# One core, gated cross-attention with a mixture of experts: four expert weight sets parked in DRAM at every second step, three split in place late

## What is computed

```python
# x: 4 x 512 x 256, ctx: 4 x 1024 x 256; 16 heads of 16; all fp32
x = x + tanh(g_xattn) * attention(layernorm(x), ctx, ctx, Wq, bq, Wk, bk, Wv, bv, Wo, bo)
x = x + tanh(g_ffn) * ffn(layernorm(x))
# ffn: 1 shared expert + 8 routed experts, top 2 of softmax(x @ gate_w + gate_b)
#   expert(z) = (silu(a) * b) @ w2 + b2,  a, b = split(z @ w1 + b1), w1: 256 x 512, w2: 256 x 256
```

## Time and profile before

| | us |
|---|---|
| median of 3 runs | 699.52 |
| the three runs | 698.99, 699.52, 710.46 |
| the profiled execution's own time | 703.27 |
| its span, first to last instruction | 701.4 |
| its mean granted TensorE clock, share of full speed | 0.963 |

### The profile page before, as it was taken

One profiled execution on the slowest core, in us unless ns is written; L12 is line 12 of the kernel. 1 busy time (PEld: TensorE's weight loads), 2 busy tenths in 40 slices (PEclk: granted clock), 3 DMA queues, 4 the chain that ended last, 5 costly groups with the idle time before them and its releaser, 6 DMA issues.

```text
span 701.4 us, 12642 instructions
## 1 busy us (share of the span) xinstructions
PE 627.2 (89%) x3577; PEld 324.4 (46%) x3577; DVE 482.6 (69%) x804; ACT 424.1 (60%) x842; POOL 281.0 (40%) x318
## 2 busy tenths in 40 slices
PE   4996867999999999999999999999986989999990
PEld 3774632333323323232233333336455768888870
DVE  4788876888887878778688888856675664444430
ACT  4775343777767767677677777786641414555540
POOL 2443242424834654464321113311037532655642
PEclk9999896999999999999999999999998999999995
DMA  8999889565587679569556745005069556665645
GB/s 239 359 263 369 174 266 179 88 106 108 121 218 204 154 153 229 170 116 250 138 83 80 105 66 161 1 13 229 2 219 317 187 196 140 100 104 101 94 46 142
DMA packets 83607, 110.29 MB, mean 157 GB/s; under 512 B 16798, under 2 KB 64841, under 8 KB 82604
## 3 DMA queue, kind: packets, MB, share of 16 engines
q1 hardware_dynamic: 70268, 78.34, 47.3%
q0 software_dynamic: 13296, 31.42, 17.6%
HBM read 64.19 MB, written 47.34 MB: 159 GB/s over the span
## 4 chain that ended last, share of the span: by engine, by line
PE 64%; issue 12%; DMA 8%; POOL 6%; DVE 6%; ACT 1%; POOLq 1%; another core or an unknown queue 0%; SPq 0%; ACTq 0%; DVEq 0%
PE psO L1535 15%; PE psS L1508 15%; PE psM L1490 12%; PE psH L1752 8%; DMA kq<-msb 6%; PE psY L1778 4%; POOL parts L603 3%; PE psH L1709 2%; PE psX L1603 1%; PE psX L1741 1%; PE psH L1763 1%; POOL kq L596 1%; PE psO L1578 1%; PE psM L1508 1%; DMA wA_raw<-wqkv 1%
## 5 line engine op out<-in xcount | busy, mean ns | idle before, releaser
L1142 DVE TENSOR_REDUCE mneg<-psM 128x1 f32<-128x1024 f32 x240 | 282.7, 1219 | 73.8 <-PE psM L1490 73.6
L876 ACT ACTIVATE pr<-psS 128x512 f32<-128x512 f32 x488 | 266.7, 595 | 108.0 <-PE psS L1508 107.9
L1508 PE MATMUL psS<-kq 99*128 99x512 bf16 x488 | 153.0, 387 | 12.7 <-DMA kq<-msb 12.1
L1535 PE MATMUL psO<-pr,vt 128*32 128x512 f32 x1024 | 136.9, 607 | 0.0
L1490 PE MATMUL psM<-kq 96*128 96x512 bf16 x480 | 128.5, 388 | 4.4 <-DVE mneg L1142 2.7
L1508 PEld LDWEIGHTS psS<-kq 99*128 99x128 bf16 x488 | 40.0, 97 | 161.1 <-ACT pr L876 131.3
L585 POOL TENSOR_TENSOR msb<-mcp,none 16x128 bf16<-16x128 f32 x16 | 6.2, 389 | 198.0 <-ACT mcp L853 198.0
L783 POOL DMA_INDIRECT acc<-ysb,ids x39 | 60.2, 1543 | 61.1 <-ACT ysb L999 42.6
L1490 PEld LDWEIGHTS psM<-kq 96*128 96x128 bf16 x480 | 46.7, 98 | 63.6 <-DVE mneg L1142 8.1
L1752 PE MATMUL psH<-wall,zgT 128*128 x234 | 61.0, 396 | 1.4 <-DVE zgT L1373 1.4
L1379 DVE TENSOR_TENSOR rg<-psH,rs 128x256 f32<-128x256 f32 x39 | 16.6, 425 | 57.2 <-ACT rs L987 52.7
(11 more groups left out here) (250 smaller groups left out, 845.2 us busy)
## 6 DMA issues: line engine op xcount, KB each, us to landing
kq<-k_parts SPq DMA_DIRECT2D x96, 128.0 KB, 6.4
wall<-w_parts SPq DMA_DIRECT2D x7, 1536.0 KB
w_parts<-wraw POOLq DMA_DIRECT2D x11, 768.0 KB, 4.9
v_pad<-vst SPq DMA_DIRECT2D x16, 512.0 KB, 8.6
vt<-v_pad SPq DMA_DIRECT2D x16, 512.0 KB, 10.2
k_parts<-parts SPq DMA_DIRECT2D x16, 384.0 KB, 7.1
kq<-q_parts SPq DMA_DIRECT2D x96, 64.0 KB, 6.4
zg<-zs SPq DMA_DIRECT2D x39, 136.0 KB, 2.3
```

What stands on the lines that cost most here:

```text
L876: nc.scalar.activation(pr[:, slot, j], score_bank(s, j), ACT.Exp, scale=SCALE).then_inc(e_done, 1)
L1142: V.tensor_reduce(mneg[:, parity, i:i + 1], psM[:, i % 2], X_AXIS, ALU.max, negate=True).then_inc(m_free, 1)
L1508: mm(score_bank(s, j), kst[:, slot, j, kt * P:(kt + 1) * P], qst[:, slot, j], start=True, stop=True).then_inc(s_full, 1)
L1535: last = mm(psO[j * VW:(j + 1) * VW, u % 2], vt[:, u, k, j * VW:(j + 1) * VW], pr[:, k % 4, j], start=(k == 0), stop=(k == KT - 1), skip_g ...
```

## The change

Of the seven late experts, 3 to 6 are still parked (`PARKED`), but in iterations 3, 5, 7 and 9, with the raw load of the next one in iterations 4, 6 and 8; one raw buffer serves. Experts 0 to 2 (`PLACED`) are no longer parked: in the last batch SP loads them raw into the slot of `kq` that has just come free (`place`), over all 128 partitions, and POOL splits them there in iterations 13 and 14 and after the loop (`split_placed`), the low part in place. `w_at` turns the slots accordingly, and the table has one DVE instruction more. `blank_rows` moves to iteration 12, and its two DMAs of SP go to POOL's queue. Nothing else is changed.

```diff
+PLACED = 3
+PARKED = LATE - PLACED
...
-        sR = ExitStack()
-        sb("raw_shift", [P, QT * D], F32, sR)
-        raw2 = sb("raw2", [P, WCOLS], F32, sR)
-        sR.close()
...
+        placed_raw = nc.alloc_sbuf_tensor_at("placed_raw", [P, PLACED, 2 * WCOLS], F32, offset=kq_at)
...
-            return LU + WU * e if e < LATE else WU * (e - LATE)
+            return LU + WU * ((e + LATE - NG) % LATE) if e < LATE else WU * (e - LATE)
...
+            def late_weights(e):
+
+                n = e - PLACED
+                if n:
+                    sp.wait_ge(wl_ld, 16 * n)
                 sp.dma_start(wall[:, w_at(e):w_at(e) + WU].rearrange("p u c -> p (u c)").bitcast(F32),
-                             w_parts[e]).then_inc(wl_ld, 16)
+                             w_parts[n]).then_inc(wl_ld, 16)
+
+            def place(e):
+
+                raw, row = placed_raw[:, e, WCOLS:2 * WCOLS], placed_raw[:, e, 0:2 * FF]
+                sp.dma_start(raw, wexp[raw_of(e)]).then_inc(pl_ld[e], 16)
+                sp.dma_start(row, wexp[raw_of(e), P - 1:P, 2 * FF:4 * FF].to_broadcast([P, 2 * FF])).then_inc(pl_ld[e], 16)
...
-            sp.wait_ge(wp_st, 32 * LATE)
             for u in range(NG):
+                unit_dmas(NB - 1, u, True)
+                if u:
+
+                    sp.wait_ge(s_full, HG * KT * (UNITS - NG + u))
+                    place(u - 1)
                 if u == 2:
                     load_output(1)
-                unit_dmas(NB - 1, u, True)
-                if u:
-
-                    sp.wait_ge(s_full, HG * KT * (UNITS - NG + u))
-                    late_weights(LATE - NG + u - 1, u - 1)
-                if u == 2:
                     load_output(2)
             sp.wait_ge(s_full, HG * KT * UNITS)
-            late_weights(LATE - 1, NG - 1)
+            sp.wait_ge(wp_st, 32 * PARKED)
+            late_weights(PLACED)
 
             sp.wait_ge(pv_done, 4 + KT * UNITS)
             sp.wait_ge(bp_st, 16 * 3)
             sp.wait_ge(b2_ok, 1)
             sp.dma_start(b2_sh[0:3], b2_parts[:, NR * D:NE * D]).then_inc(b2_in, 16)
-            late_weights(0, NG)
+            late_weights(PLACED + 1)
             sp.wait_ge(o_taken, UNITS + 1)
             sp.wait_ge(at_full, NB)
-            for e in range(1, LATE - NG):
-                late_weights(e, NG + e)
-
-            sp.wait_ge(fill_ok, 2)
-            spare_rows = zs[NR * REGION:SLOTS].rearrange("(k p) c -> p k c", p=P)
-            sp.dma_start(spare_rows[:, :, 0:264], fill[:, 0:264].unsqueeze(1).to_broadcast([P, SPARES, 264])).then_inc(fill_st, 16)
-            sp.dma_start(spare_rows[:, :, 264:272], spare_ids).then_inc(fill_st, 16)
+            late_weights(PLACED + 2)
+            late_weights(PLACED + 3)
...
-            sp.wait_ge(fill_st, 16 * (2 + NR))
+            sp.wait_ge(fill_st, 16 * NR)
+            sp.wait_ge(blank_st, 32)
...
-            def stage(e):
-
-                raw, hi = raw_at(e), wraw[:, 1]
-                pool.wait_ge(raw_ld[0], 16 * (2 + e))
-                less_last_row(1 + e, e, raw)
-                if e:
-
-                    pool.wait_ge(wp_st, 32 * e)
+            def raw_in(q):
+
+                if q:
+                    pool.wait_ge(wp_st, 32 * q)
+                nc.gpsimd.dma_start(wraw[:, 0], wexp[raw_of(PLACED + q)]).then_inc(raw_ld[0], 16)
+                last_row_in(1 + q, PLACED + q)
+
+            def stage(q):
+
+                raw, hi = wraw[:, 0], wraw[:, 1]
+                pool.wait_ge(raw_ld[0], 16 * (2 + q))
+                less_last_row(1 + q, PLACED + q, raw)
                 nc.gpsimd.tensor_copy(hi.bitcast(F32R), raw).then_inc(wp_hi, 1)
-                pool.wait_ge(wp_hi, e + 1)
+                pool.wait_ge(wp_hi, q + 1)
                 nc.gpsimd.tensor_tensor(raw.bitcast(F32R), raw, hi, ALU.subtract).then_inc(wp_ok, 1)
-                pool.wait_ge(wp_ok, e + 1)
-                nc.gpsimd.dma_start(w_parts[e, :, 0:WCOLS], hi).then_inc(wp_st, 16)
-                nc.gpsimd.dma_start(w_parts[e, :, WCOLS:2 * WCOLS], raw).then_inc(wp_st, 16)
-                if e + 1 < LATE:
-                    raw_in(e + 1)
-
-            def raw_in(e):
-
-                nc.gpsimd.dma_start(raw_at(e), wexp[raw_of(e)]).then_inc(raw_ld[0], 16)
-                last_row_in(1 + e, e)
+                pool.wait_ge(wp_ok, q + 1)
+                nc.gpsimd.dma_start(w_parts[q, :, 0:WCOLS], hi).then_inc(wp_st, 16)
+                nc.gpsimd.dma_start(w_parts[q, :, WCOLS:2 * WCOLS], raw).then_inc(wp_st, 16)
+
+            def split_placed(e):
+
+                hi, lo = w_half(e, 0), w_half(e, 1)
+                raw, row = placed_raw[:, e, WCOLS:2 * WCOLS], placed_raw[:, e, 0:2 * FF]
+                pool.wait_ge(pl_ld[e], 32)
+                nc.gpsimd.dma_start(raw[P - 1:P, 2 * FF:4 * FF], b1_rows[raw_of(e):raw_of(e) + 1]).then_inc(b1_ld, 16)
+                nc.gpsimd.tensor_tensor(raw[:, 0:2 * FF], raw[:, 0:2 * FF], row, ALU.subtract).then_inc(pl_c, 1)
+                nc.gpsimd.tensor_tensor(raw[0:P - 1, 2 * FF:4 * FF], raw[0:P - 1, 2 * FF:4 * FF], row[0:P - 1], ALU.subtract).then_inc(pl_c, 1)
+                pool.wait_ge(pl_c, 3 * e + 2)
+                pool.wait_ge(b1_ld, 16 * (2 + PARKED + e))
+                nc.gpsimd.tensor_copy(hi, raw).then_inc(pl_c, 1)
+                pool.wait_ge(pl_c, 3 * e + 3)
+                nc.gpsimd.tensor_tensor(lo, raw, hi.bitcast(F32), ALU.subtract).then_inc(wl_pos, 1)
+
+            def blank_rows():
+
+                pool.wait_ge(wp_st, 32 * PARKED)
+                nc.gpsimd.memset(fill, 0.0).then_inc(fill_c, 1)
+                pool.wait_ge(fill_c, 1)
+                nc.gpsimd.tensor_copy(fill[:, 264:272].bitcast(U32), spare[:, 0:1].to_broadcast([P, 8])).then_inc(fill_ok, 1)
+                nc.gpsimd.tensor_copy(spare_ids.bitcast(U32), spare[:, 1:1 + SPARES].unsqueeze(2).to_broadcast([P, SPARES, 8])).then_inc(fill_ok, 1)
+                pool.wait_ge(fill_ok, 2)
+                nc.gpsimd.dma_start(acc[NB * NQ:].rearrange("(k p) d -> p k d", p=P),
+                                    fill[:, 0:D].unsqueeze(1).to_broadcast([P, 1 + SPARES, D])).then_inc(added, 16)
+                spare_rows = zs[NR * REGION:SLOTS].rearrange("(k p) c -> p k c", p=P)
+                nc.gpsimd.dma_start(spare_rows[:, :, 0:264], fill[:, 0:264].unsqueeze(1).to_broadcast([P, SPARES, 264])).then_inc(blank_st, 16)
+                nc.gpsimd.dma_start(spare_rows[:, :, 264:272], spare_ids).then_inc(blank_st, 16)
 
             for n in range(UNITS - 1):
                 if n >= UNITS - NG:
@@ -714,8 +739,10 @@
                 split_max(n + 1, (n + 1) % 2)
                 if n == EARLY:
                     load_tail()
-                elif n == 2 + LATE:
+                elif n == 10:
                     scale_bias()
+                elif n == 12:
+                    blank_rows()
                 if n < EARLY:
 
                     pool.wait_ge(raw_ld[n], 16)
@@ -723,14 +750,18 @@
                         last_row_in(0, NE - 2)
                     else:
                         less_last_row(0, NE - 2, wraw[:, 1])
-                    if n == 1:
                         pool.wait_ge(bp_st, 48)
                     prepare(n, NE - 1 - n, n)
                     if n == 1:
                         raw_in(0)
-                elif n < 2 + LATE:
-                    stage(n - 2)
+                elif n in (3, 5, 7, 9):
+                    stage((n - 3) // 2)
+                elif n in (4, 6, 8):
+                    raw_in((n - 2) // 2)
+                elif n >= UNITS - 3:
+                    split_placed(n - UNITS + 3)
             bias_x(NB - 1)
+            split_placed(PLACED - 1)
...
-            pool.wait_ge(wp_st, 32 * LATE)
-            nc.gpsimd.memset(fill, 0.0).then_inc(fill_c, 1)
-            pool.wait_ge(fill_c, 1)
-            nc.gpsimd.tensor_copy(fill[:, 264:272].bitcast(U32), spare[:, 0:1].to_broadcast([P, 8])).then_inc(fill_ok, 1)
-            nc.gpsimd.tensor_copy(spare_ids.bitcast(U32), spare[:, 1:1 + SPARES].unsqueeze(2).to_broadcast([P, SPARES, 8])).then_inc(fill_ok, 1)
-            pool.wait_ge(fill_ok, 2)
-            nc.gpsimd.dma_start(acc[NB * NQ:].rearrange("(k p) d -> p k d", p=P),
-                                fill[:, 0:D].unsqueeze(1).to_broadcast([P, 1 + SPARES, D])).then_inc(added, 16)
...
-                link(V.tensor_scalar(at, e_f, LATE - 0.5, -float(LU + LATE * WU), ALU.is_gt, ALU.mult))
-                link(V.tensor_scalar(at, at, float(LU), None, ALU.add))
+                early = room[:, TAB * NR:TAB * NR + TAB]
+                V.tensor_scalar(early, e_f, LATE - 0.5, -float(LU + WU * PLACED), ALU.is_gt, ALU.mult)
+                link(V.tensor_scalar(at, e_f, PLACED + 0.5, -float(LATE * WU), ALU.is_gt, ALU.mult))
+                link(V.scalar_tensor_tensor(out=at, in0=at, scalar=float(LU + WU * PLACED), in1=early, op0=ALU.add, op1=ALU.add))
...
-            pe.wait_ge(wl_ld, 16 * LATE)
+            pe.wait_ge(wl_pos, PLACED)
```

(1 more changed line is left out.)

16 lines of the change are left out of this document (6 added, 10 removed).

## The result

Over 20 runs of each on one chip the changed kernel has a median of 696.5 us (691.28 to 700.76) and the kernel before 701.26 us (695.76 to 713.99). The ratio is 0.9945, with a 95% interval of 0.9918 to 0.9972: no change by the 2% mark, and faster by 0.5%. The medians differ by 4.8 us where 9.7 were forecast, and 696.5 us is the upper end of the forecast's range (686.0 to 696.5). The ratios in this document compare only the runs within 1.5% of the fastest of their kernel and group, while the medians are of all runs. The profiled run took 695.57 us (span 693.7) against 703.27 (span 701.4). I cut both spans at POOL's first `split_max` instruction of a unit and at POOL's first memset behind attention.

A forecast was written before the change was run, and what follows sets the result against it. TensorE was taken as the bound, waiting for late strips. 11.0 us excess less 0.3 and 0.2, +0.1, gave -10.4; without the low clock 8.8; taking 9.7, 699.52 - 9.7 = 689.8 us, range 686.0 to 696.5.

The forecast's parts named there:

- Staging and raw loads apart: Attention, nine periods: separating stores from loads lets strips land within the slack, removing nearly all of 11.0 us excess.
- The 0.3 us that I left for `load_tail`: Third strip of 178 us, with 384 KB right behind it: a TensorE wait of some 0.3 us stays.
- Rivals A and B: Raw loads in iterations 4, 6, 8 delay strips: partly, 693 to 696, chance 0.14; full size, 710, chance 0.03.
- "Hidden, 0" for the three placed experts: Late attention: POOL's splits and `bias_x(3)` finish before anything waits for them, cost 0; uncovered, 11 us per split.
- rival C: Router: three DVE sums wait out POOL's splits, up to 8.9 us, 698.7; a third likelier, 693; chance 0.13.
- Rival E: Between attention and tiles, 2 MB less traffic also saves 4 to 5 us: 685; chance 0.05.
- Blank rows: Moving them from behind attention to iteration 12: 0 to -1 us there, taken as 0; 0 in iteration 12.
- The reference point: Median before of 699.52 us, from which the gain of 9.7 us was subtracted.

The follow-up runs named there:

- group D: Changed kernel and variants (splits moved, split arithmetic in pieces, both) beside the kernel before on one chip: changed 716.01 us, before 717.62 us.
- held: Kernel before, with SyncE's last two weight loads held until TensorE has done the shared expert's four first hidden-layer products: 707.6 us, ratio 0.9971.
- busy POOL: Kernel before, with only the arithmetic of two splits added on POOL and no transfer added or moved: 721.36 us, ratio 1.0146.
- splits kept apart: Changed kernel, POOL's second split before its last row maximum, last bias addition directly behind that maximum's stores, third split later: 690.24 and 709.17 us.
- group C: Kernel before measured against itself, beside changed kernels with splits moved, last loads held, or both: 708.45 against 704.97 us; 690.24, 695.53, 690.97 us.

## Why the prediction was wrong, point by point

**Staging and raw loads apart: right.** The excess of nine periods was to go from 11.0 to about 0.5; it went to 211.61 - 9 x 23.52 = -0.1. The 0.3 us that I left for `load_tail` did not stay either in the changed kernel; in two of its variants in group D TensorE waited at that place, 0.7 and 1.3 us. Nine profiles of the changed kernel and its variants without the stall show 329.4 to 329.9 us for the units. The term is worth more than I could read from one profile: four of the kernel before and its variants (held, busy POOL) take 340.5, 343.3, 346.8 and 355.9 us for it, so the gain is 11 to 26 us.

**Rivals A and B: wrong.** In the changed kernel's four profiles no set of strips behind 130 us makes TensorE wait.

**"Hidden, 0" for the three placed experts: this is the step that failed.** I asked who waits for the splits and for `bias_x(3)`, and nobody does; but the splits take something from VectorE while they run. It measured +7.5 us of that stretch in the first profile, 54.07 - 46.57 (6.2 to 10.7 in four profiles of the changed kernel), and 5 to 7 us of the time. I had it as rival C at 0.13, with the Trainium skill's page beside it, and looked for it in the wrong instructions: the three large sums, which TensorE follows by 0.49 us. Those read PSUM and do not wait. The ones that wait are the small ones right behind, 0.17 us each, which my price left out. My argument against C, that VectorE was as busy beside staging passes (19.43 us a period) as without them, came from a stretch where all of its work reads PSUM; I said so in the same sentence and gave C little chance all the same. I priced it at 693 as likely and 698.7 as its end; it is near that end.

**Rival E:** the part behind attention was 4.9 us shorter in the pair of profiles, as E had it in size; the cause is another one. The first profile of the kernel before had the stall, the first of the changed one had not. Against profiles without it (178.5, 179.7) the part behind attention is unchanged (179.7 to 179.8 in three of the changed kernel). The TensorE wait of 5.9 us that I tied E to, and the low clock behind it, went with the stall: in the kernel before of group C, which has none, that wait is 1.6 us.

**Blank rows: 0 where there is no stall** (697.28 against 696.56), and perhaps 10 us the wrong way where there is, which is argued above and not shown.

**The reference point.** I subtracted from the median of three runs, 699.52. Its median over 20 runs in the comparison was 701.26 and in the groups 705 to 718. The changed kernel stood at 695.75 to 696.56 in three of the four groups in which it ran. Term by term, the sum of -10.4 should have been -11.0 for the units and +7.5 for the last units, -3.5; the medians differ by 701.26 - 696.5 = 4.8, and the remaining 1.3 lies inside what the kernel before scatters. The missed term of 7.5 us is about the difference between the forecast and what came: 689.8 + 7.5 = 697.3 against 696.5. That the two meet so closely is in part luck, as the other profiles put this term at 6.2 to 10.7 us and that of the units at 11 to 26.

The best version is the change with the splits kept apart: 690.24 us in group C (0.9849, interval 0.9788 to 0.9910, against the kernel before). In group D, with the stall, it beats the changed kernel (709.17 against 716.01) but not clearly the kernel before (0.9965, interval 0.9924 to 1.0005).
